# A bidirectional Mamba layer on one core: softplus as one ScalarE function, and four pieces of work put elsewhere in the order

## The reference

```python
xz = einsum('ed,bld->bel', in_proj_w, xn)            # 512 channels: x part, z part
# for each direction (the second sees the tokens reversed, own weights):
u = silu(causal_conv4(x_part) + conv_bias)           # 256 channels
x_dbl = einsum('bdl,kd->bkl', u, xproj_w)            # 8 step rows, 16 B rows, 16 C rows
delta = softplus(dtproj_w @ x_dbl[:, :8] + dt_bias)
dA  = exp(delta * A)                                 # A = -exp(A_log), 256 x 16
dBx = delta * B * u
h[t] = dA[t] * h[t-1] + dBx[t]                       # per channel and state
y = (sum over the 16 states of h * C + Dp * u) * silu(z)
out_mamba = out_proj_w @ (y_forward + y_backward)
# linear layer: xh = xn @ H (Hadamard); 4-bit rounding of each row of xh; ternary weight
out = x + out_mamba + xq @ wq.T
```

## Time and profile before

| what | value |
|---|---|
| median of 3 runs | 885.19 us (882.79 to 886.7) |
| the profiled execution | 887.24 us, span 885.2 us |
| granted TensorE clock, mean over the span | 0.941 |
| busy: PE, DVE, ACT, POOL | 757.5, 798.4, 779.7, 729.3 us |
| DVE scans (line 627) | 512, 581.7 us |
| POOL products (line 752) | 255, 598.6 us |
| start of the first and the last DVE correction (line 602) | 67.7 and 796.8 us |

### The profile page before, as it was taken

The page is one execution under the profiler, slowest core; times in us unless marked ns, Lnnn a source line. Parts: engine busy times, 40 slices in busy tenths (PEclk is TensorE's granted clock), DMA queues, the critical chain, the costliest instruction groups (busy, mean ns, idle before and its releaser), DMA issues. The chain is left out here.

```text
span 885.2 us, 12125 instructions
## 1 busy us (share of the span) xinstructions
PE 757.5 (86%) x3953; PEld 390.4 (44%) x3953; DVE 798.4 (90%) x855; ACT 779.7 (88%) x1436; POOL 729.3 (82%) x355
## 2 busy tenths in 40 slices
PE   8867978799897988989799798979989897997885
PEld 6324445253543535344363445435353443634353
DVE  3849899998999999998999989999999989999996
ACT  2699997999979998999989999899989999898870
POOL 0176979798896988889697888979888896978994
PEclk9978999989999999999999999999999999999797
DMA  6435126070441608143180614506071430706100
GB/s 182 124 73 143 37 79 127 3 179 4 120 94 38 145 4 188 31 109 70 38 181 4 162 21 104 112 32 151 4 178 39 104 76 33 174 3 154 26 25 13
DMA packets 55119, 74.83 MB, mean 85 GB/s; under 512 B 6784, under 2 KB 23568, under 8 KB 55056
## 3 DMA queue, kind: packets, MB, share of 16 engines
q1 hardware_dynamic: 54624, 73.79, 35.7%
q10 hardware_dynamic: 432, 0.26, 0.1%
HBM read 62.49 MB, written 11.53 MB: 84 GB/s over the span
## 5 line engine op out<-in xcount | busy, mean ns | idle before, releaser
L752 POOL TENSOR_TENSOR hst<-hst,c_rep 128x1024 f32<-128x1024 f32 x255 | 598.6, 2372 | 103.0 <-DVE hst L627 90.6
L627 DVE TENSOR_TENSOR_SCAN hst<-da,b_ps 128x512 f32<-128x512 f32 x512 | 581.7, 1199 | 27.1 <-issue 21.0
L433 ACT ACTIVATE da<-rep,neg_a 128x511 f32<-128x511 f32 x504 | 331.5, 709 | 6.0 <-DVE hst L627 5.8
L964 PE MATMUL b_ps<-ident,dbx_t 128*128 128x128 f32 x1536 | 238.6, 296 | 97.0 <-DVE hst L627 72.5
L964 PEld LDWEIGHTS b_ps<-ident,dbx_t 128*128 128x128 f32 x1536 | 181.6, 150 | 225.1 <-DVE hst L627 130.4
L420 ACT ACTIVATE dbx_t<-du_t,b_t 128x256 f32<-128x256 f32 x576 | 248.1, 495 | 2.6 <-PE b_ps L964 1.9
L985 PE MATMUL y<-hst,sum_sel 128*32 128x512 f32 x1024 | 149.3, 658 | 4.3 <-POOL hst L752 4.3
L869 PE MATMUL pb<-xnt,conv_wt 128*128 128x512 f32 x240 | 110.7, 604 | 1.6 <-ACT du_t L403 0.9
L762 POOL TENSOR_TENSOR dbx_t<-du_t,b_t 128x1024 f32<-128x1024 f32 x48 | 91.7, 1910 | 7.6 <-ACT du_t L403 7.6
L943 PE MATMUL b_ps<-t_log,spread_sel 32*128 32x512 f32 x256 | 88.8, 666 | 1.7 <-DVE hst L627 1.0
L616 DVE TENSOR_TENSOR b_ps<-b_ps,b_rep 128x1024 f32<-128x1024 f32 x64 | 77.9, 1218 | 3.6 <-PE b_ps L943 2.3
(11 more groups left out here) (135 smaller groups left out, 602.8 us busy)
## 6 DMA issues: line engine op xcount, KB each, us to landing
rep<-d_scr SPq DMA_DIRECT2D x128, 256.0 KB, 9.1
c_rep<-bc_scr SPq DMA_DIRECT2D x64, 256.0 KB, 4.8
d_scr<-t_pos SPq DMA_DIRECT2D x16, 512.0 KB, 3.0
b_rep<-bc_scr SPq DMA_DIRECT2D x64, 64.0 KB, 2.4
x_ln<-x SPq DMA_DIRECT2D x8, 256.0 KB, 3.3
x_res<-x SPq DMA_DIRECT2D x8, 256.0 KB, 3.0
out<-x_res SPq DMA_DIRECT2D x8, 256.0 KB, 7.5
rep<-x SPq DMA_DIRECT2D x7, 256.0 KB, 4.4
```

The lines of the kernel that those rows point to most:

```text
L433: nc.scalar.activation(da[s % 2][:, j, 1:L], rep[d][h][:, j, 1:L], ACT.Exp, scale=neg_a[:, d, h, j, q:q + 1]).then_inc(decay_done, 1)
L627: nc.vector.tensor_tensor_scan(hst[s % RING][:, j, :], da[s % 2][:, j, :], b_ps[:, j, :], 0.0, ALU.mult, ALU.add).then_inc(scan_done, 1)
L752: nc.gpsimd.tensor_tensor(hst[s % RING][:, two, :], hst[s % RING][:, two, :], c_rep[d][:, q:q + 1, :].broadcast_to([P, 2, L]), ALU.mult).t ...
L964: ins = tr(b_ps[:, j, P * c:P * (c + 1)], dbx_t[(NX * d + q - 1) % 2][:, c, NJ * h + j, :, :].rearrange("p r e -> p (r e)"), ident[:, :])
```

## The change

- Softplus is one ScalarE function. `softplus` does two passes of 512 columns, each from the PSUM bank to `t_pos`; they stand in slot 2 where Abs and Relu stood. Exp, Copy, Ln and the three DVE operations are gone. `u_sigmoid` then need not wait for the old delta, but for u.
- `du` has a buffer of its own (it was `t_log`), and `make_du` waits for the replicas of the old one.
- POOL's product for q = 3 stands in slot 3, behind `make_du`, and not in slot 4. PE's skip products (Dp times u) of d = 0, half 1 stand in slot 2 and not in slot 3; POOL's small `scales` moves ahead by what stood before it.
- The start: 16 warming matmuls for 32; the first softplus is two passes; the second convolution's taps are spread between the replicas; logarithm and exponential for the other batches' norms, and their refinement on POOL, come in slots 2 and 3 of the first unit (statistics are kept in another buffer).
- The end: DVE gates half 0 of y before its last product with C, not behind it.

```diff
@@ ScalarE
-            def softplus_in(d, V):
+            def softplus(d, V):
                 wait(act, u_ready, 2 * V + 2)
                 wait(act, delta_stored, DMA * V)
                 wait(act, du_ready, V)
                 for n, h in enumerate((1, 0)):
                     act.wait_ge(dt_filled, 2 * V + n + 1)
-                    nc.scalar.activation(t_exp[:, h, :], pb[:, h, :], ACT.Abs, bias=col[:, d, 1, h:h + 1]).then_inc(sp_step, 1)
-                    nc.scalar.activation(t_pos[:, h, :], pb[:, h, :], ACT.Relu, bias=col[:, d, 1, h:h + 1]).then_inc(sp_step, 1)
+                    ins = nc.scalar.activation(t_pos[:, h, :], pb[:, h, :], ACT.Softplus, bias=col[:, d, 1, h:h + 1])
+                ins.then_inc(delta_ready, 1)
...
-                    if s == 3:
-                        if nxt:
-                            softplus_log(V)
...
                     if s == 2 and nxt:
-                        softplus_in(e, V)
+                        softplus(e, V)
+                        if U == 0:
+                            log_var(1, slice(NC, NB * NC))
+                            guess_rstd(1, slice(NC, NB * NC))
@@ VectorE
-                    if s == 2 and nxt:
-                        log1p(V)
...
-                    if s == 2 and nxt:
-                        delta(V)
...
             batches(dve, body)
+            gate_y(NB - 1, 0)
             dve.wait_ge(scan_done, NJ * PER_B * NB)
             nc.vector.tensor_tensor(hst[RING - 1][:, 2:NJ, :], hst[RING - 1][:, 2:NJ, :], c_rep[1][:, NQ - 1:NQ, :].broadcast_to([P, 2, L]), ALU.mult).then_inc(last_prod, 1)
-            gate_y(NB - 1, 0)
             gate_y(NB - 1, 1)
@@ GpSimd
-                    if s == 3 and nxt:
-                        make_du(e, V)
-                    if s == 4:
-                        if d == 1:
-                            max_known(b)
+                    if s == 3:
+                        if nxt:
+                            make_du(e, V)
                         inputs_free(U, 3)
                         inputs_t(d, 3)
-                        if d == 1:
-                            scales(b)
+                    if s == 4 and d == 1:
+                        max_known(b)
+                        scales(b)
@@ TensorE
-            warm(32)
+            warm(16)
...
                     if s == 2:
-                        skip_products(b, d, (0,) if d == 0 else (0, 1))
+                        skip_products(b, d)
...
-                            skip_products(b, d, (1,))
```

More of the change, by code:

```diff
@@ L95, in build @@
         x_all = [rep[1][n][:, :, :].rearrange("p b (c d) -> p b c d", c=NC) for n in range(2)]
-        stats = hst[3][:, 3, 0:6 * NB * NC].rearrange("p (t k) -> p t k", k=6)
-        msum, mdiff, var = [hst[3][:, 3, 6 * NB * NC + NB * NC * n:6 * NB * NC + NB * NC * (n + 1)] for n in range(3)]
+        stats = y_gated[:, 1, 0:6 * NB * NC].rearrange("p (t k) -> p t k", k=6)
+        msum, mdiff, var = [y_gated[:, 1, 6 * NB * NC + NB * NC * n:6 * NB * NC + NB * NC * (n + 1)] for n in range(3)]
         b_ps = ps("b_ps", [P, NJ, L])
@@ L341, in u_sigmoid @@
                 act.wait_ge(conv_filled, 2 * V + h + 1)
-                wait(act, delta_ready, V)
+                wait(act, u_ready, 2 * V)
                 source = y[:, h, :] if V == 1 else pb[:, 1 - h, :]
@@ L388, in first_decays @@
                     nc.scalar.activation(da[h][:, j, 1:L], pb[:, j % 2, 1:L], ACT.Exp, scale=neg_a[:, 0, h, j, 0:1]).then_inc(decay_done, 1)
-            def softplus_log(V):
-                act.wait_ge(sp_step, 6 * V + 4)
-                nc.scalar.activation(t_exp[:, :, :], t_exp[:, :, :], ACT.Exp, scale=-1.0).then_inc(sp_step, 1)
-                act.wait_ge(sp_step, 6 * V + 5)
-                nc.scalar.activation(pb[:, :, :], t_exp[:, :, :], ACT.Copy, bias=1.0).then_inc(sp_step, 1)
-                act.wait_ge(sp_step, 6 * V + 6)
-                wait(act, t_filled, NJ * (SLOTS * (V - 1) + NH))
-                wait(act, dut_filled, 2 * V)
-                nc.scalar.activation(t_log[:, :, :], pb[:, :, :], ACT.Ln).then_inc(log_ready, 1)
             def keep_dut(d, V, n):
@@ L819, in _ @@
             inputs_t(0, 1)
-            refine(slice(NC, NB * NC))
             def unit(b, d):
@@ L827, in unit @@
                 for s in range(SLOTS):
+                    if s == 3 and U == 0:
+                        refine(slice(NC, NB * NC))
                     states_times_c(b, d, s, 0)
@@ L965, in inputs, with skip_products @@
                     ins.then_inc(t_filled, 1)
-            def skip_products(b, d, hs):
+            def skip_products(b, d):
                 step = slice(None, None, -1 if d else 1)
                 pe.wait_ge(u_ready, 2 * (2 * b + d) + 2)
-                for h in hs:
-                    mm(y[:, h, :], skip[:, d, h, :], u[d][:, h, step], start=False, stop=False, skip_group_check=True)
+                for h in range(NH):
+                    if d == 0 and h == 1:
+                        wait(pe, y_read, 2 * b)
+                    mm(y[:, h, :], skip[:, d, h, :], u[d][:, h, step], start=d == 0 and h == 1, stop=False, skip_group_check=True)
             def sum_states(b, d, s):
@@ L976, in sum_states @@
                 step = slice(None, None, -1 if d else 1)
-                if q == 0 and d == 0:
-                    wait(pe, y_read, 2 * b - 1 + h)
+                if s == 0 and d == 0:
+                    wait(pe, y_read, 2 * b - 1)
                 if last(b) and d == 1 and s == SLOTS - 1:
@@ L1017, in _ @@
             step_replicas(0, (2, 3))
-            pe.wait_ge(delta_ready, 1)
             copies(0, 0, 1)
-            step_replicas(1, range(NJ))
+            conv(1, 1, 0, range(2, TAPS), weights_ready, 2)
+            step_replicas(1, (0, 1))
+            conv(1, 1, 1, range(2), weights_ready, 2)
+            step_replicas(1, (2, 3))
+            conv(1, 1, 1, range(2, TAPS), weights_ready, 2)
             du_transposed(0, 0, decay_done, 2 * NJ)
```

64 lines of the change are left out of this document (11 added, 53 removed).

## The result

The changed kernel takes 835.63 us, median of 4 runs (832.82 to 836.41), against 884.53 us (882.79 to 886.7) for the kernel before on the same chip. The ratio is 0.944, 95% interval 0.9409 to 0.9472. The forecast was 820 us with a range of 798 to 845. The profiled execution took 835.33 us with a span of 833.5.

A forecast was written before the change was run, and what follows sets the result against it. A loop through DVE, POOL and PE, 96.1 us a batch, was to set the pace above each engine's own 91. Span 885.2 - 52 (14 periods) - 12 (start) - 1.5 (end) = 819.7, forecast 820 us, range 798 to 845.

The forecast's parts named there:

- The loop: DVE's slot 7 to slot 1 scans, POOL's products, PE's sum, convolution and transposes: 47.7 and 48.4 us a unit.
- Rival 1: No loop forms and the fullest engine sets the unit, 45.7 us: 782 us; chance 0.09, with all between 782 and 799.
- Its size: Middle units: the period falls from 52.1 to 48.4 us, 52 us less over 14 periods.
- 0.8 for the clock: PE at half clock in sum and convolution: between 0 and 4.6 us, put at 0.4 us a unit.
- Rival 3: Clock falls at the convolution in every unit, loop 52.6 us at worst; 847 us with half the units; chance 0.17.
- The rule of the clock: PE's idle-and-recover rule taken alone would put the loop's added cost nearer 4.6 us than 0.5.
- The start: First unit: earlier transposes, du and B products bring slot 3's scans from 73.46 to near 61 to 62, 12 us earlier.
- The q = 3 move: POOL's product a slot sooner: alone 1.7 of DVE's 3.83 us rest; within the loop, included in either slot.
- Costs put at nothing: Middle units: skip products in PE's slot 2, POOL's scales, u_sigmoid's and make_du's waits cost nothing.
- ACT: Middle units: ACT saves 4.5 us net a unit, which buys nothing as such, only an earlier delta.
- The end: After the last product: final sum starts 2.4 us sooner, POOL's lag takes perhaps 1 us; 1.5 us in all.

The follow-up runs named there:

- the idle matmuls: Changed kernel plus one to two zero matmuls on PE ahead of the sums of slots 3 and 4, where PE waits for POOL: 831.44 us, ratio 0.9424.
- the two start kernels: Changed kernel plus eight idle matmuls before the first du, 830.57 us; changed kernel with the second convolution in one piece ahead of the replicas, 830.35 us.
- the last kernel: Changed kernel with second convolution in one piece ahead of replicas, zero matmuls before sums of slots 3 and 4, two more in the last unit: 826.08 us.

## Why the prediction was right, and where it was off

- **The loop.** Right in its mechanism, and in its length to 1 us in 97. Its legs were forecast as 17.5 (its own terms add up to 17.6), 24.9 and 5.3 us into a backward unit and measured 17.8, 25.1 and 5.3; into a forward one 18.2, 24.9 and 5.3, measured 18.8, 24.6 and 5.7. POOL's added work is paid in full, that of DVE and ACT is not. PE waits for POOL ahead of `sum_states`, for 41.9 us in 21 waits. Rival 1, no loop, fell with the same rows.
- **Its size.** 14 periods were to give 52 us and gave (796.8 - 67.7) - (759.3 - 72.8) = 42.6. A batch was put at 96.1 us plus 0.8 for the clock. It is 96.9 with the clock up throughout and 97.7 in the same five batches of the changed kernel; its first is longer, 98.9. So 0.8 us a batch is the clock, shown by the idle matmuls, and that term was right. The mis-sized term is the length of the legs, 0.8 us a batch short; the 0.23 us scale is part of it, the rest was not taken apart. Rival 3's mechanism is in the result at a fraction of its size: the fall comes earlier than it said, at the transposes behind the wait for slot 3's product, and the convolution runs at full clock (3.70 us).
- **The rule of the clock.** The Trainium skill (TensorE: Matmul & The Clock Gate, "Part 1: The HAM clock gate") says that TensorE falls back to 1.2 GHz when it was idle and gets 2.4 GHz back only after staying busy. The trace agrees on the fall (2.64 us of wait, then 1.92 for 1.03). The price of up to 4.6 us a unit that it might have had here came out near 0.4.
- **The start.** Mis-sized: 12 us forecast, 73.46 - 66.3 = 7.2 measured. The forecast's 30 us for the first B product was right to 0.5 us, and it had the second convolution give back 2.8 us. It gave back all 7.2: u of the second unit starts at 47.19. Of the missing 4.4 us the rows show 4.2 as half clock over four taps (3.78 and 3.47 us for 1.98 each) and two replicas (2.08 for 1.13); the two start kernels won 2.9 and 3.6 us back. With u no sooner than before, the 7.2 us to slot 3's scans are the first unit's own gain behind it.
- **The q = 3 move.** Alone it gave 1.1 to 1.6 us a batch where 1.7 was forecast. Wrong was that within the loop its place makes no difference. Taking it back costs 29.5 us there, more than all other edits give without it (18.3): with it in slot 4 PE's transposes stand between POOL's product and the sum, behind a wait after which the clock is at half.
- **Costs put at nothing.** The skip products and `make_du`'s wait cost nothing that a row shows. The scales make the reciprocal wait 1.6 us; the time did not change when they were moved, so nothing was right for the sum, and the place of the backward unit's rest was wrong (forecast 2.1 us ahead of slot 7, found 1.6 at the reciprocal).
- **ACT.** That its saved work (64.5 us in all) buys nothing as such is borne out as far as it was tried: 12.6 us put back cost 3.5, within the spread of the runs, and nothing in the middle batches. The rest of it was not put back. Softplus at 0.69 us a pass was right (0.684).
- **The end.** 1.5 us forecast. The sum closes with it: 51.7 us of span less 7.2 and 42.4 to the same scans of the last unit but one leave 2.1. (The medians differ by 48.9 only, as the profiled execution of the kernel before was 2.7 us above its median.)

The range held mostly because the loop's length was built from three legs of the trace before, with the clock as its upper side. The span exceeded 819.7 us by 13.8: 4.8 at the start, 9.6 in the 14 periods, and 0.6 less at the end. Raising the clock at the start and in the loop takes 9.7 us off the span. What the rest is made of was not taken apart further; the first batch, 98.5 us even in the last kernel, is some 1.6 of it.

## What to carry to other kernels

When four engines are all at 85 to 90%, add up the round trip through them, with what stands in front in each queue, and compare that with each engine's own need; then test it by giving each engine a little useless work. An operation moved a slot earlier on one engine is worth what the engine that waits for it then finds in front of its next critical instruction. The wait in the profile does not tell it: the kernel before lists 17.1 us of PE waiting for POOL's `dbx_t`, and the same move was worth 7.6 us in that kernel and 29.5 in the changed one. A long wait on an engine with slack may be only the place where the loop's slack shows, and removing it moves it.
